# Four-block vision kernel: seven instead of six of sixteen scan states per tile have their input product on GpSimd, and the output evacuation moves behind the C copy of state 3

## The chip, the cores and the metric

The kernel runs on one core of a Trainium2 chip. The metric is the device time of one execution in microseconds (us), given as the median of several runs. Profiles come from one execution taken by the hardware profiler.

## What is computed

Four blocks follow each other on an image batch x of 4 x 32 x 32 x 32, each with a normalization in front and a residual sum behind: a deformable 3x3 convolution, a 7x7 neighbourhood attention, a three-direction selective scan (Mamba), and a convolution whose result is the sampling grid of a bilinear gather. The change touches only the third. Its core, cut from the reference:

```python
def mamba_dir(xz, conv_w, conv_b, x_proj_w, dt_w, dt_b, A_log, Dp):
    ...
    delta = softplus(einsum('dr,brl->bdl', dt_w, dt_raw) + dt_b)
    A = -exp(A_log)
    # for each of 16 states n, along the sequence l of 1024:
    #   h = h * exp(delta * A[n]) + (delta * u) * B[n];  y += h * C[n]
    y = selective_scan(x, delta, A, Bm, Cm) + Dp * x
    return y * silu(z)
```

## The kernel before, in words

Each engine has its own hand-written instruction stream, and the streams meet at counting semaphores; no scheduler reorders anything. The scan stage works through six tiles k = 0 to 5 (`DP`), three directions for each of two pairs of batch elements, in the order of `ORDER`. A tile is 128 rows by 1024 positions, and for each of its 16 states n (`NS`) the following happens:

- TensorE (`spread`, L880) replicates the rows B[n] and C[n] over the partitions with two 128x512 matmuls each. It does so for state n+4 before it sums state n (`AHEAD`, L939).
- ScalarE (loop at L1725) computes the decay exp(delta*A[n]) (L1729) and copies C out of PSUM banks 4 and 5 into a ring of four (L1742).
- VectorE multiplies du = delta*u with the B row in PSUM (`inject`, L1373, recorded at the helper's line L1061) and runs the recurrence as one scan instruction (`scan`, L1378, recorded at L1388).
- GpSimd (loop at L1877, all its multiplies recorded at L1789) multiplies the scan's result with C into a ring of four.
- TensorE (`collect`, L900) adds that product, transposed in eight matmuls, to the output y in banks 6 and 7.

States listed in `SHARED` (L63) go another way: their B row is replicated into the same banks 4 and 5 that the C rows use (`b_share`, L894, two states ahead), ScalarE copies it to SBUF (L1747), and GpSimd does the product with du, three states ahead (L1888). VectorE then has no `inject` for this state, only the scan. Banks 4 and 5 thus pass from TensorE to ScalarE once for each C row and once more for each shared B row, and each waits for the other at every passing. Two buffers hold shared products (`slot_free`, L78).

Extra work stands at fixed states. At state 8 ScalarE scales u by D (the "skip", L1752), which takes one more slot of the ring that the products go through. In tiles 0 to 2 GpSimd also computes du for a later tile behind state 7 (L1892). In tiles 1, 3 and 4 (`copy_y`, L1722) ScalarE evacuates the previous tile's output from banks 6 and 7 at state 3; in tiles 1 and 4 TensorE then transposes it back (`turn_back`, L924, matmuls at L929), ScalarE copies that in natural order at state 4 (L1738) and TensorE collects the copy (`collect_third`, L933).

Of the kernel before, what the change touches and what calls it, by code (L numbers as in the profile page):

```python
# [23 lines left out]
T = C * C  # L24
# [28 lines left out]
DI, NS, KC, RANK = 64, 16, 4, 2  # L53
DIRS, PAIRS = 3, 2
# [5 lines left out]
CGRP, CPER = 4, 8  # L60


SHARED = (3, 6, 8, 11, 13, 15)  # L63
NSH = len(SHARED)


ORDER = [PAIRS * dr + p for p in range(PAIRS) for dr in (2, 0, 1)]
# [5 lines left out]
def item(k, what):  # L73

    return ITEMS.index((k, what))


def slot_free(k, j):  # L78

    if j >= 2:  # L80
        return k * NS + SHARED[j - 2] + 1
    return (k - 1) * NS + SHARED[NSH - 1 - j] + 1


def injected(n):

    return sum(m not in SHARED for m in range(n + 1))

# [29 lines left out]
def above(n):  # L118
    return n + LEAD
# [17 lines left out]
def build(nc, d, out):  # L137
    with ExitStack() as ctx:
# [3 lines left out]
        def sem(name):  # L142
            return ctx.enter_context(nc.semaphore(name))
# [4 lines left out]
        def bank2(i):  # L148
            return ps[:, i:i + 2, :].rearrange("p a n -> p (a n)")
# [211 lines left out]
        def S(name):  # L361
            if name not in s:
                s[name] = sem(name)
            return s[name]
# [211 lines left out]
        def _(pe):  # L576
# [303 lines left out]
            def spread(k, n):  # L880

                t = ORDER[k]
                if n not in SHARED:
                    pe.wait_ge(S("scan"), above(k * NS + (n - 1)))
# [3 lines left out]
                pe.wait_ge(S("c_copied"), above(k * NS + n))  # L888
                if n + 1 in SHARED:
                    pe.wait_ge(S("b_copied"), above(k * NSH + SHARED.index(n + 1) + 1))  # L890
# [610 lines left out]
        def _(ac):  # L1501
# [40 lines left out]
            for k in range(TAPS):  # L1542
# [18 lines left out]
                if k in (2, 3):  # L1561

                    flat, n = off_px.rearrange("p c k n -> p (c k n)"), NBLK * NOFF // 3
# [158 lines left out]
            def copy_y(t, cols):  # L1722
                ac.activation(du[:, t, cols], bank2(6)[:, cols], ACT.Copy).then_inc(S("y_turned"), 1)

            for k in range(DP):  # L1725
                t = ORDER[k]
                for n in range(NS):
                    ac.wait_ge(S("scan"), above(k * NS + (n - 1)))
                    ac.activation(bank2(2 * (n % 2)) if n in SHARED else da[:, n % 2], delta[:, t], ACT.Exp,  # L1729
                                  scale=a_all[:, t * NS + n:t * NS + n + 1]).then_inc(S("da"), 1)  # L1730
                    if n == 3 and k in (1, DIRS, DIRS + 1):
                        ac.wait_ge(S("y_acc"), above(item(k - 1, NS - 1) + 1))
                        copy_y(0 if k == DIRS else ORDER[k - 1], slice(0, T))
                    if n == 4 and k % DIRS == 1:
                        q = item(k, "third")
                        ac.wait_ge(S("y_back"), 2 * (k // DIRS + 1))
                        ac.wait_ge(S("y_acc"), above(q - RING + 1))
                        ac.activation(hc_ring[q % RING].rearrange("p (s m) -> p s m", s=SLICES),  # L1738
                                      bank2(6).rearrange("p (m s) -> p s m", s=SLICES), ACT.Copy).then_inc(S("y_natural"), 1)
                    ac.wait_ge(S("c_rep"), above(k * NS + (n + 1)))  # L1740
                    ac.wait_ge(S("hc"), above(k * NS + (n - RING + 1)))
                    ac.activation(c_ring[n % RING], bank2(4), ACT.Copy).then_inc(S("c_copied"), 1)  # L1742
                    if n + 2 in SHARED:
                        j = SHARED.index(n + 2)
                        ac.wait_ge(S("b_share"), above(k * NSH + (j + 1)))
                        ac.wait_ge(S("scan"), above(slot_free(k, j)))
                        ac.activation(dbu_sh[j % 2], bank2(4), ACT.Copy).then_inc(S("b_copied"), 1)  # L1747
                    if n == SKIP_AT:
                        q = item(k, "skip")
                        ac.wait_ge(S("y_acc"), above(q - RING + 1))  # L1750
                        step = -1 if t // PAIRS == 1 else 1
                        ac.activation(hc_ring[q % RING], u[:, t // PAIRS, t % PAIRS, ::step], ACT.Copy,  # L1752
                                      scale=d_col[:, t // PAIRS, t % PAIRS:t % PAIRS + 1]).then_inc(S("skip"), 1)
# [271 lines left out]
```

## Time and profile before

| what | us |
|---|---|
| median of 3 runs (lowest, highest) | 751.73 (746.66, 754.73) |
| the profiled execution: its own time | 747.03 |
| the profiled execution: span from first to last instruction | 745.2 |
| busy over the span: VectorE, TensorE, ScalarE, GpSimd | 651.0, 605.2, 504.7, 418.9 |
| scan stage, 300.6 to 599.0: length | 298.4 |
| busy in it: VectorE, GpSimd, ScalarE, TensorE | 284.7, 262.3, 236.2, 209.8 |

In rows of the trace DVE is VectorE, ACT is ScalarE, POOL is GpSimd, PE is TensorE. A timeline row is: start in us from the span's start, length in us, engine, line, operation, output<-inputs, shape, count, and in brackets the idle time of the engine before it and what ended it. Instructions are pipelined, so the distance from one start to the next is often shorter than a length; the prediction goes by distances between starts. "PEclk" is the granted clock of TensorE as a share of 2.4 GHz.

### The profile page before, as it was taken

The numbers are of one execution on the slowest core, as the hardware profiler recorded it, in microseconds if no ns is written. First come the engines' busy times: TensorE is split into PE (matmuls) and PEld (weight loads), VectorE is DVE, ScalarE is ACT, GpSimd is POOL, SyncE is SP. The second block draws the span as 40 slices with busy tenths as digits, with TensorE's granted clock in tenths as the row PEclk, the third lists the DMA queues.
The fourth block names the chain that finished last, engine by engine and source line by source line (L and its number), as shares of the span: only waits on it lengthen the run. The fifth ranks groups of instructions, "written<-read, shape, count | busy, mean of one in ns | idle before, by whom it ended". The sixth has DMA issues, their size and how long they took to land.

```text
span 745.2 us, 11671 instructions
## 1 busy us (share of the span) xinstructions
PE 605.2 (81%) x3947; PEld 345.9 (46%) x3947; DVE 651.0 (87%) x900; ACT 504.7 (68%) x604; POOL 418.9 (56%) x288
## 2 busy tenths in 40 slices
PE   7899998999997971567676776777757789899997
PEld 5555545677774420245444454454434553333332
DVE  7899996879985979999999999999999874888876
ACT  2657531879984777688787787888877710577673
POOL 3788873000001067699899898798997920622321
PEclk9999999999999995599999898899997999899999
DMA  2004200341001032000000000000000013100000
GB/s 58 5 13 100 34 1 1 71 95 31 4 4 61 14 74 49 1 0 1 1 0 1 0 1 1 0 1 1 0 2 0 1 33 70 43 1 1 14 1 14
DMA packets 28853, 14.98 MB, mean 20 GB/s; under 512 B 23022, under 2 KB 24942, under 8 KB 28654
## 3 DMA queue, kind: packets, MB, share of 16 engines
q1 hardware_dynamic: 27582, 13.61, 8.3%
q10 hardware_dynamic: 1216, 0.66, 0.4%
q8 instruction: 32, 0.52, 0.3%
q14 instruction: 23, 0.19, 0.1%
HBM read 5.14 MB, written 0.78 MB: 8 GB/s over the span
## 4 chain that ended last, share of the span: by engine, by line
DVE 40%; PE 37%; ACT 10%; issue 9%; POOL 3%; DMA 0%; DVEq 0%; SPq 0%; ACTq 0%; POOLq 0%
PE ps L580 34%; DVE arena L1388 15%; DVE ps L1061 8%; DVE arena L1107 4%; DVE arena L1061 4%; ACT arena L1628 3%; ACT arena L1742 2%; DVE ps L1107 2%; PE ps L762 1%; DVE arena L1275 1%; POOL arena L1789 1%; DVE arena L1339 1%; ACT ps L1729 1%; PE ps L641 1%; ACT arena L1729 1%
## 5 line engine op out<-in xcount | busy, mean ns | idle before, releaser
L580 PE MATMUL ps<-arena 128*32 128x64 f32 (+5 forms) x2072 | 334.5, 350 | 111.1 <-ACT arena L1742 33.1
L580 PEld LDWEIGHTS ps<-arena 128*32 128x32 f32 (+4 forms) x2072 | 122.0, 123 | 242.4 <-issue 93.1
L1789 POOL TENSOR_TENSOR arena<-arena 128x1024 f32<-128x1024 f32 x87 | 173.8, 2012 | 32.3 <-DVE arena L1388 10.7
L1388 DVE TENSOR_TENSOR_SCAN arena<-arena,ps 128x1024 f32<-128x1024 f32 x60 | 137.2, 2286 | 8.2 <-DVE ps L1061 0.5
L1774 ACT ACTIVATE arena<-ps,nycol 128x1024 f32<-128x1024 f32 x64 | 71.1, 1113 | 55.3 <-PE ps L580 55.3
L1061 DVE TENSOR_TENSOR ps<-arena,ps 128x1024 f32<-128x1024 f32 x69 | 83.6, 1212 | 4.9 <-PE ps L580 3.9
L1388 DVE TENSOR_TENSOR_SCAN arena<-ps,arena 128x1024 f32<-128x1024 f32 x36 | 81.6, 2268 | 0.2
L1729 ACT ACTIVATE arena<-arena,a_col 128x1024 f32<-128x1024 f32 x60 | 68.6, 1144 | 10.9 <-DVE arena L1388 10.6
L1910 POOL TENSOR_TENSOR arena<-arena,bmask 128x128 f32<-128x128 f32 x64 | 30.7, 482 | 76.4 <-PE ps L580 65.3
L1061 DVE TENSOR_TENSOR arena<-ps,arena 128x512 f32<-128x512 f32 (+2 forms) x75 | 48.6, 654 | 23.5 <-PE ps L580 18.5
L1628 ACT ACTIVATE arena<-arena 128x256 f32<-128x256 f32 x128 | 59.0, 503 | 6.2 <-DVE arena L1275 4.7
L580 PE MATMUL ps<-ident,arena 128*128 128x128 f32 x416 | 58.8, 289 | 0.8 <-POOL arena L1789 0.8
L580 PEld LDWEIGHTS ps<-ident,arena 128*128 128x128 f32 x416 | 53.4, 151 | 11.8 <-issue 3.1
L1852 POOL MEMSET arena<- 128x6 f32 (+1 forms) x3 | 0.2, 101 | 101.0 <-DVE x2t L1302 101.0
L1747 ACT ACTIVATE arena<-ps 128x1024 f32<-128x1024 f32 x36 | 37.0, 1027 | 28.3 <-PE ps L580 28.3
L1742 ACT ACTIVATE arena<-ps 128x1024 f32<-128x1024 f32 x48 | 49.0, 1022 | 7.2 <-PE ps L580 7.1
L1275 DVE CUSTOM_DVE_ANT_0 arena<-ps,w_conv 128x256 f32<-128x256 f32 x124 | 50.9, 414 | 0.0
L1460 DVE TENSOR_SCALAR arena<-arena 128x1024 f32<-128x1024 f32 x64 | 46.9, 735 | 0.3 <-ACT arena L1774 0.3
L1729 ACT ACTIVATE ps<-arena,a_col 128x1024 f32<-128x1024 f32 x36 | 40.2, 1117 | 5.7 <-DVE arena L1388 5.7
L580 PE MATMUL ps<-arena,w_attn 96*128 96x512 bf16 (+1 forms) x132 | 42.5, 407 | 1.8 <-ACT arena L1774 0.9
L762 PE MATMUL ps<-ident,arena 128*128 128x128 f32 x256 | 38.4, 283 | 3.7 <-ACT arena L1628 2.3
L1107 DVE SCALAR_TENSOR_TENSOR arena<-ps,arena 128x1024 f32<-128x1024 f32 x32 | 37.0, 1217 | 3.1 <-ACT arena L1539 2.6
(208 smaller groups left out, 1016.4 us busy)
## 6 DMA issues: line engine op xcount, KB each, us to landing
arena<-arena SPq DMA_DIRECT2D x54, 64.0 KB
arena<-arena SPq DMA_DIRECT2D x12, 128.0 KB, 3.3
w_conv<-in_c_far SPq DMA_DIRECT2D x1, 1152.0 KB, 5.7
w_conv<-rpb_pad SPq DMA_DIRECT2D x36, 28.0 KB, 1.8
arena<-x SPq DMA_DIRECT2D x12, 64.0 KB, 2.0
arena<-x1t SPq DMA_DIRECT2D x12, 64.0 KB, 2.0
arena<-x3t SPq DMA_DIRECT2D x12, 64.0 KB, 2.0
arena<-arena SPq DMA_DIRECT2D x2, 288.8 KB, 3.7
```

Source lines behind the costliest of these rows:

```text
L580: return pe.matmul(o, l, r, start=start, stop=stop, **k)
L762: last = pe.transpose(ps[:, PT_BANKS[q % 2], side + P * c:side + P * c + P], pexp[:, (GROUP * g + e) % NRING, P * c:P * c + P], ident[:])
L1061: return ve.tensor_tensor(o, a, b, op)
L1107: return ve.scalar_tensor_tensor(out=square(o), in0=square(dx), scalar=0.0, in1=of, op0=sign, op1=ALU.mult)
L1275: ve.tensor_tensor_reduce(sc[:, n % NSB], ps[:, SC_BANKS[q % len(SC_BANKS)], SPAN * (e % 2):SPAN * (e % 2) + SPAN], bias(m, kind_of(i)), 1 ...
L1388: ve.tensor_tensor_scan(hs_ring[n % RING], decay, add, 0.0, ALU.mult, ALU.add).then_inc(S("scan"), 1)
L1460: ve.tensor_scalar(nhat[:, t % NU], ahat[:, t % NU], 1.0, 1.0, ALU.min, ALU.subtract).then_inc(S("nhat"), 1)
L1628: ac.activation(pexp[:, n % NRING], sc[:, n % NSB], ACT.Exp, bias=nmax[:, n % NSB:n % NSB + 1], scale=-1.0).then_inc(S("pexp"), 1)
L1729: ac.activation(bank2(2 * (n % 2)) if n in SHARED else da[:, n % 2], delta[:, t], ACT.Exp, scale=a_all[:, t * NS + n:t * NS + n + 1]).then ...
L1742: ac.activation(c_ring[n % RING], bank2(4), ACT.Copy).then_inc(S("c_copied"), 1)
L1774: ac.activation(ahat[:, t % NU].rearrange("p q n -> p (q n)"), bank2(2 * (t % 2)), ACT.Abs, bias=nycol[:, 0:1]).then_inc(S("abs"), 1)
L1789: return gp.tensor_tensor(o, a, b, ALU.mult)
```

## The change

`SHARED` gets seven states, every odd one from 3 on, instead of six, and in ScalarE's stream the evacuation of y (`copy_y`) at state 3 moves from ahead of the C copy to behind it.

```diff
-SHARED = (3, 6, 8, 11, 13, 15)
+SHARED = (3, 5, 7, 9, 11, 13, 15)
...
-                    if n == 3 and k in (1, DIRS, DIRS + 1):
-                        ac.wait_ge(S("y_acc"), above(item(k - 1, NS - 1) + 1))
-                        copy_y(0 if k == DIRS else ORDER[k - 1], slice(0, T))
...
                     ac.activation(c_ring[n % RING], bank2(4), ACT.Copy).then_inc(S("c_copied"), 1)
+                    if n == 3 and k in (1, DIRS, DIRS + 1):
+                        ac.wait_ge(S("y_acc"), above(item(k - 1, NS - 1) + 1))
+                        copy_y(0 if k == DIRS else ORDER[k - 1], slice(0, T))
```

ScalarE at states 3 to 5 of the fifth tile (k = 4), before: L1729 is a decay, L1723 the evacuation, L1742 a C copy, L1738 the copy in natural order, L1747 a copy of a shared B row.

```order
L1729 ACTIVATE ps<-arena,a_col 128x1024 [waits scan]
L1723 ACTIVATE arena<-ps 128x1024 [waits y_acc]
L1742 ACTIVATE x1t<-ps 128x1024 [waits hc,c_rep]
L1729 ACTIVATE arena<-arena,a_col 128x1024 [waits scan]
L1738 ACTIVATE arena<-ps 128x1024 [waits y_acc,y_back]
L1742 ACTIVATE arena<-ps 128x1024 [waits hc,c_rep]
L1747 ACTIVATE arena<-ps 128x1024 [waits scan,b_share]
```

The same place now (C copies are at L1739, the copy in natural order at L1735).

```order
L1729 ACTIVATE ps<-arena,a_col 128x1024 [waits scan]
L1739 ACTIVATE x1t<-ps 128x1024 [waits hc,c_rep]
L1723 ACTIVATE arena<-ps 128x1024 [waits y_acc]
L1747 ACTIVATE arena<-ps 128x1024 [waits scan,b_share]
L1729 ACTIVATE arena<-arena,a_col 128x1024 [waits scan]
L1735 ACTIVATE arena<-ps 128x1024 [waits y_acc,y_back]
L1739 ACTIVATE arena<-ps 128x1024 [waits hc,c_rep]
L1729 ACTIVATE ps<-arena,a_col 128x1024 [waits scan]
```

The evacuation stands behind the C copy of state 3, and the copy of a shared B row (that of state 5) now stands behind the evacuation; the one behind the C copy of state 4 (it was that of state 6) is gone.

TensorE at the start of the same tile, from the spread of state 3 to the spread of state 4, before: 128x512 pairs are replicated rows, 128x128 groups with "waits hc" a collect, those at L929 the turn-back.

```order
L580 MATMUL ps<-arena 128x512 [waits c_copied]
L580 MATMUL ps<-arena 128x512
L580 MATMUL ps<-ident,arena 128x128 [waits hc]
L580 MATMUL ps<-ident,arena 128x128 x7
L929 MATMUL ps<-ident,arena 128x128 [waits y_turned]
L929 MATMUL ps<-ident,arena 128x128 x7
L580 MATMUL ps<-arena 128x512 [waits scan]
```

The same place now.

```order
L580 MATMUL ps<-arena 128x512 [waits c_copied]
L580 MATMUL ps<-arena 128x512
L580 MATMUL ps<-arena 128x512 [waits c_copied]
L580 MATMUL ps<-arena 128x512
L580 MATMUL ps<-ident,arena 128x128 [waits hc]
L580 MATMUL ps<-ident,arena 128x128 x7
L929 MATMUL ps<-ident,arena 128x128 [waits y_turned]
L929 MATMUL ps<-ident,arena 128x128 x7
L580 MATMUL ps<-arena 128x512 [waits scan]
```

The shared B row of state 5 came in between the C row of state 3 and the collect of the previous tile's state 15, and it waits for the C copy of state 3, which the collect now waits for too.

GpSimd at states 0 to 5 of the second tile, before: rows that wait for "b_copied" are products of shared states, the others products with C.

```order
L1789 TENSOR_TENSOR x3t<-arena 128x1024 [waits c_copied,y_acc,scan,du_pool]
L1789 TENSOR_TENSOR arena<-arena 128x1024 [waits b_copied]
L1789 TENSOR_TENSOR xn<-arena 128x1024 [waits y_acc,c_copied,scan]
L1789 TENSOR_TENSOR arena<-arena,x 128x1024 [waits y_acc,c_copied,scan]
L1789 TENSOR_TENSOR arena<-arena,x1t 128x1024 [waits y_acc,c_copied,scan]
L1789 TENSOR_TENSOR arena<-arena 128x1024 [waits b_copied]
L1789 TENSOR_TENSOR x3t<-arena 128x1024 [waits y_acc,c_copied,scan]
```

The same place now.

```order
L1789 TENSOR_TENSOR x3t<-arena 128x1024 [waits c_copied,y_acc,scan,du_pool]
L1789 TENSOR_TENSOR arena<-arena 128x1024 [waits b_copied]
L1789 TENSOR_TENSOR xn<-arena 128x1024 [waits y_acc,c_copied,scan]
L1789 TENSOR_TENSOR arena<-arena,x 128x1024 [waits y_acc,c_copied,scan]
L1789 TENSOR_TENSOR arena<-arena 128x1024 [waits b_copied]
L1789 TENSOR_TENSOR arena<-arena,x1t 128x1024 [waits y_acc,c_copied,scan]
L1789 TENSOR_TENSOR x3t<-arena 128x1024 [waits y_acc,c_copied,scan]
L1789 TENSOR_TENSOR arena<-arena 128x1024 [waits b_copied]
```

From state 0 to state 12 a shared product now follows every second product with C.

## Rows read from the trace of the kernel before

**Rows 1.** Groups by line of VectorE, 299 to 600 us: busy, mean ns, idle before

```profile
L1061 DVE TENSOR_TENSOR ps<-arena,ps 128x1024 f32<-128x1024 f32 x60 | 72.6, 1210 | 4.3 <-PE ps L580 3.9
```

**Rows 2.** Timeline of VectorE: scan of state 0 of each tile, and last scan

```profile
300.58 2.29 DVE L1388 TENSOR_TENSOR_SCAN arena<-arena,ps 128x1024 f32<-128x1024 f32 x1
...
350.13 2.29 DVE L1388 TENSOR_TENSOR_SCAN arena<-arena,ps 128x1024 f32<-128x1024 f32 x1
...
399.71 2.29 DVE L1388 TENSOR_TENSOR_SCAN arena<-arena,ps 128x1024 f32<-128x1024 f32 x1
...
449.16 2.29 DVE L1388 TENSOR_TENSOR_SCAN arena<-arena,ps 128x1024 f32<-128x1024 f32 x1
...
499.23 2.29 DVE L1388 TENSOR_TENSOR_SCAN arena<-arena,ps 128x1024 f32<-128x1024 f32 x1
...
548.04 2.29 DVE L1388 TENSOR_TENSOR_SCAN arena<-arena,ps 128x1024 f32<-128x1024 f32 x1
...
596.65 2.28 DVE L1388 TENSOR_TENSOR_SCAN arena<-ps,arena 128x1024 f32<-128x1024 f32 x1
```

**Rows 3.** Timeline of VectorE: shared scan 11, product 12, shared scan 13, tile 0

```profile
335.17 2.26 DVE L1388 TENSOR_TENSOR_SCAN arena<-ps,arena 128x1024 f32<-128x1024 f32 x1
337.35 1.21 DVE L1061 TENSOR_TENSOR ps<-arena,ps 128x1024 f32<-128x1024 f32 x1
...
340.89 2.26 DVE L1388 TENSOR_TENSOR_SCAN arena<-ps,arena 128x1024 f32<-128x1024 f32 x1
```

**Rows 4.** Timeline of all engines: GpSimd's product for state 13 and its scan, tile 3

```profile
487.68 2.00 POOL L1789 TENSOR_TENSOR arena<-arena 128x1024 f32<-128x1024 f32 x1
...
489.64 2.00 POOL L1789 TENSOR_TENSOR arena<-arena,x1t 128x1024 f32<-128x1024 f32 x1
489.81 2.29 DVE L1388 TENSOR_TENSOR_SCAN arena<-ps,arena 128x1024 f32<-128x1024 f32 x1
```

**Rows 5.** Timeline, full clock: decay and C copy 6, shared B row, next rows

```profile
366.75 1.11 ACT L1729 ACTIVATE ps<-arena,a_col 128x1024 f32<-128x1024 f32 x1
...
367.78 1.01 ACT L1742 ACTIVATE x<-ps 128x1024 f32<-128x1024 f32 x1
...
368.86 0.60 PE L580 MATMUL ps<-arena 96*128 96x512 bf16 x2 [1.34 <-ACT x L1742]
...
369.50 1.03 ACT L1747 ACTIVATE arena<-ps 128x1024 f32<-128x1024 f32 x1 [0.70 <-PE ps L580]
...
370.17 1.09 PE L580 MATMUL ps<-arena 96*128 96x512 bf16 x4
```

**Rows 6.** Timeline, low clock: shared B row, next rows, product of state 10

```profile
377.46 0.76 PE L580 MATMUL ps<-arena 96*128 96x512 bf16 x2 [1.52 <-ACT arena L1742]
...
379.72 1.76 PE L580 MATMUL ps<-arena 96*128 96x512 bf16 x4
...
380.82 1.23 DVE L1061 TENSOR_TENSOR ps<-arena,ps 128x1024 f32<-128x1024 f32 x1 [0.25 <-PE ps L580]
```

**Rows 7.** Busy time by windows; behind POOL's come PEclk, DMA share, GB/s

```profile
377.80:381.20 3.40, 3.40 (x14) 2.33 (x13) 3.02 (x3) 2.06 (x2) 3.22 (x3) 0.50 0.00 0
```

**Rows 8.** Timeline of all engines, tile 4: decay 3, evacuation, turn-back, rows 4 and 5

```profile
505.16 1.11 ACT L1729 ACTIVATE ps<-arena,a_col 128x1024 f32<-128x1024 f32 x1
...
505.76 1.04 PE L580 MATMUL ps<-ident,arena 128*128 128x128 f32 x8
...
506.84 1.03 ACT L1723 ACTIVATE arena<-ps 128x1024 f32<-128x1024 f32 x1 [0.56 <-PE ps L580]
...
507.92 1.09 PE L929 MATMUL ps<-ident,arena 128*128 128x128 f32 x8 [1.12 <-ACT arena L1723]
...
508.85 1.03 PE L580 MATMUL ps<-arena 96*128 96x512 bf16 x4
...
513.88 1.03 PE L580 MATMUL ps<-arena 96*128 96x512 bf16 x4
...
514.52 1.23 DVE L1061 TENSOR_TENSOR ps<-arena,ps 128x1024 f32<-128x1024 f32 x1 [0.20 <-PE ps L580]
```

## The prediction

> **What bounds the kernel now.** I read the busy shares first, then the scan stage by engine, then single states. VectorE leads the busy shares, and the scan stage, where the change lies, keeps it busy almost throughout: the path runs there. In that stage its 60 input products cost 1.21 us each, and nearly all idle time ahead of them, 3.9 us, ended with a replicated row from TensorE [rows 1]. Next, the cadence of VectorE: from a shared scan to the next instruction 337.35 - 335.17 = 2.18 us, for a product with its scan 340.89 - 337.35 = 3.54 [rows 3]. A tile of ten unshared and six shared states needs 10 x 3.54 + 6 x 2.18 = 48.48. The first five tiles took 548.04 - 300.58 = 247.46, so they lost 247.46 - 5 x 48.48 = 5.06, about 1.0 each; I take the same for the sixth, 6.1 in all [rows 2].
>
> The other engines are close behind. GpSimd starts a multiply every 489.64 - 487.68 = 1.96 us, and VectorE's scan of a shared state follows 0.17 behind the end of its product (489.64 to 489.81): in the second half of this tile GpSimd, not VectorE, already came last [rows 4].
>
> **What the change takes away.** One product per tile leaves VectorE: 9 x 3.54 + 7 x 2.18 = 47.12, that is 1.36 per tile and 8.2 us over six tiles, if nothing else comes late. TensorE replicates as many rows as before. ScalarE gets one more B copy per tile and GpSimd one more multiply, both meant to lie beside VectorE's scans. Whether they do is the question.
>
> **What it adds on GpSimd.** In the alternation of shared and unshared states, VectorE needs 2.18 + 3.54 = 5.72 per pair, GpSimd 3 x 1.96 = 5.88. It starts a tile with some lead and loses 0.16 per pair. From the end of scan 2 to scan 11 VectorE needs four shared and four unshared states, 4 x 2.18 + 4 x 3.54 = 22.88. GpSimd has seven products with C (states 2 to 8) and four shared ones (5, 7, 9, 11): 11 x 1.96 plus two handovers of 0.17 is 21.9, in time. In tiles 0 to 2 the multiply for a later tile's du stands behind state 7: 23.9, so scan 11 comes 1.0 late, and the two pairs behind it lose 0.16 each. That makes 1.3 for a tile where nothing else is later: tile 2, and tile 0 (where I add 0.2 for its slow start). Tile 5 has no du multiply: 0.1.
>
> **What it adds between ScalarE and TensorE.** C rows and shared B rows pass through the same two banks in turn. At full clock, from a C copy's start to TensorE's next row 368.86 - 367.78 = 1.08, on to the B copy 0.64, and from the B row to the next state's B row, behind a collect, 370.17 - 368.86 = 1.31 [rows 5]; from that row to VectorE's product 514.52 - 513.88 = 0.64 [rows 8]. A pair costs ScalarE 1.72 from C copy to B copy and four more instructions of about 1.03 (decay 366.75 to 367.78 [rows 5]): 5.84, less some overlap of neighbours, about VectorE's 5.72. So lateness in this chain is not made up before state 14, whereas today the unshared pairs 4, 5 and 9, 10 give it room.
>
> **What it moves.** The evacuation has to stand behind the C copy of state 3 now: it waits for the collect of the previous tile's state 15, which TensorE issues behind the shared row of state 5, and that row waits for this C copy. In tile 4, counted from the scan of state 0 at 499.23 [rows 2]: decay 3 starts at 505.16, that is 5.93 [rows 8]; the C copy at 7.0; the B row of state 5 at 8.1 (+1.08); the collect 0.4 later, 8.5; the evacuation at 9.6 (505.76 to 506.84: 1.08); turn-back at 10.6 (506.84 to 507.92: 1.08); row of state 4 at 11.6 (0.93); its product at 12.2 (0.64). VectorE is ready for it after three unshared and one shared state less the first product, 499.23 + 11.47 = 510.70 by the cadence, so it waits 0.7. Queued behind the evacuation on ScalarE are the B copy of state 5, decay 4 and the copy in natural order; behind the turn-back on TensorE all later rows. The natural copy at 12.5 lets the third collect start at 13.5, the C row of state 5 at 15.3, its copy at 15.9, the B row of state 7 at 17.0, the row of state 6 at 18.3 and its product at 19.0, where VectorE would be at 17.9: another 1.0. Behind the skip at state 8 the same steps bring the row of state 10 about 0.8 late, decay 9 about 0.2, GpSimd's product for state 11 another 0.2, and the last two pairs 0.3. Together 3.2 for each of tiles 1 and 4 (in tile 1 the du multiply lies beside these waits). Tile 3 has the evacuation without the turn-back: the B copy of state 5 comes 1.8 late, and by the same steps VectorE loses 0.25 at state 6, 0.15 at decay 9, 0.8 at state 10, 0.2 at scan 11 and 0.3 in the last pairs, 1.7.
>
> **The clock.** At 377.80 to 381.20 the granted clock was 0.50, that is 1.2 GHz [rows 7]; just before, TensorE had waited 1.52 for a C copy [rows 6]. There, from the B row to the next row it took 379.72 - 377.46 = 2.26 instead of 1.31, and from there to the product 1.10 instead of 0.64 [rows 6]: 1.41 a round. Such stretches are part of the 1.0 lost per tile today; since nothing now catches up behind them, I add 2.0 for the stage, between 0 (the added B row at state 3 fills a pause of TensorE) and 8.5 (one more such round in every tile).
>
> **Sum.** Stalls after: 1.5 + 3.2 + 1.3 + 1.7 + 3.2 + 0.1 + 2.0 = 13.0, against 6.1 before: 6.9 given back out of 8.2, so -1.3. The profiled execution took 747.03, so 745.7. The median of the three runs is 4.7 above it, which I keep: 750.4. Everything outside the scan stage is unchanged.
>
> **Rivals.** Full gain: the chains run ahead as far as today, the stalls stay at 6.1 and the whole 8.2 is kept: 751.73 - 8.2 = 743.5. For it speaks that VectorE's only long waits are for TensorE's rows at unshared states, and state 5 has no such row any more; against it the cadence of GpSimd, above VectorE's in every pair. Chance 0.15.
>
> Slower: the clock falls twice in every tile. In the regular alternation TensorE stops before each shared B row until ScalarE has copied C, and these pauses recur in every pair; if TensorE falls to 1.2 GHz for two rounds per tile, that costs 12 x 1.41 = 16.9, 14.9 beyond my 2.0: 765.3. It decides from about six rounds beyond the allowance (6 x 1.41 = 8.5). For it speaks the low stretch of [rows 7], behind the skip's delay, a place that stays; against it that TensorE has as many rows to write in less time. The Trainium skill, "TensorE: Matmul & The Clock Gate", section "A second HAM failure mode: psum-queue depth-cycling", describes just this, short pauses between groups that cycle through PSUM banks making the clock swing; by that rule it would happen everywhere, while the row shows one stretch. Chance 0.14.
>
> GpSimd bound in all tiles: the ring of products holds its multiply of state 8 back in tiles 3 to 5 as the du multiply does in tiles 0 to 2. Then tiles 3 and 5 lose 1.3 more each, 753.0. For it speaks that scan 13 came behind GpSimd already in tile 3 [rows 4]; against it that the lead of 22.88 over 21.9 is there. Chance 0.13.
>
> **How the numbers follow.** The forecast has the remaining 0.58, with an own range of 746 to 755. A measurement of this kernel can tell about 1% from no change, that is below 744.2 or above 759.3. The full gain lies just below the first bound and counts about half, with a little from the forecast's edge: 0.10. The slower rival counts nearly whole, with a little of the forecast's upper edge: 0.15. The rest, 0.75, is within 1%. The range of 741 to 760 leaves out the larger part of the clock rival and a case where the old stalls go too.
>
> **What would show it.** In the changed profile: 54 input products instead of 60; tiles 1 and 4 longer than before, by about 48.81 to 49.58 before against 50.3, tiles 0, 2, 3 and 5 shorter by about a microsecond or more; a wait for TensorE ahead of the products of states 4 and 6 in tiles 1 and 4 and of state 10; scans 11, 13 and 15 behind GpSimd in tiles 0 and 2. I am wrong if tiles 1 and 4 get shorter, if all six lose or gain alike, or if low-clock stretches of TensorE spread over whole tiles.

## The result and the profile after

| what | us |
|---|---|
| before, median of 4 runs (lowest, highest) | 749.9 (746.66, 754.73) |
| after, median of 4 runs (lowest, highest) | 759.41 (756.78, 760.52) |
| after, the profiled execution: its own time, and its span | 760.52, 758.7 |

The ratio is 1.0136, with an interval from 1.0104 to 1.0167: the change makes the kernel slower by 1.4%. The profiled execution before took 747.03, so the two profiles are 13.5 apart. VectorE's tile starts, as in [rows 2], say where; the columns are start, length, engine and so on.

```profile
300.33 2.29 DVE L1388 TENSOR_TENSOR_SCAN arena<-arena,ps 128x1024 f32<-128x1024 f32 x1
...
351.65 2.29 DVE L1388 TENSOR_TENSOR_SCAN arena<-arena,ps 128x1024 f32<-128x1024 f32 x1
...
403.52 2.29 DVE L1388 TENSOR_TENSOR_SCAN arena<-arena,ps 128x1024 f32<-128x1024 f32 x1
...
452.25 2.29 DVE L1388 TENSOR_TENSOR_SCAN arena<-arena,ps 128x1024 f32<-128x1024 f32 x1
...
505.71 2.29 DVE L1388 TENSOR_TENSOR_SCAN arena<-arena,ps 128x1024 f32<-128x1024 f32 x1
...
557.98 2.29 DVE L1388 TENSOR_TENSOR_SCAN arena<-arena,ps 128x1024 f32<-128x1024 f32 x1
...
606.64 2.28 DVE L1388 TENSOR_TENSOR_SCAN arena<-ps,arena 128x1024 f32<-128x1024 f32 x1
```

| tile | 0 | 1 | 2 | 3 | 4 | 5, to its last scan | sum |
|---|---|---|---|---|---|---|---|
| before | 49.55 | 49.58 | 49.45 | 50.07 | 48.81 | 48.61 | 296.07 |
| predicted, the 2.0 for the clock left aside | 48.6 | 50.3 | 48.4 | 48.8 | 50.3 | | |
| after | 51.32 | 51.87 | 48.73 | 53.46 | 52.27 | 48.66 | 306.31 |

The scan stage is 10.2 longer, and the worst tile is 3. The other 3.5 or so lie behind it: from the last scan to the end it was 148.6 before and 152.1 after. They come up again at the end, where edits of the kernel before, with its six shared states, show a longer last stage too. Of the four tiles that the forecast had a microsecond or so shorter (0, 2, 3 and 5), only tile 2 is, by 0.7; tiles 0 and 3 got longer by 1.8 and 3.4.

The group of VectorE's input products, which answers to [rows 1], and its waits in the same stretch (waiting tensor and line, releaser, us in total, times, longest):

```profile
L1061 DVE TENSOR_TENSOR ps<-arena,ps 128x1024 f32<-128x1024 f32 x54 | 65.6, 1214 | 19.9 <-PE ps L580 19.7
```

```profile
DVE ps L1061 <- PE ps L580: 19.7, 14, 2.8
...
DVE arena L1388 <- ACT arena L1729: 0.9, 1, 0.9
```

Six products are gone, as meant. But the idle time ahead of those that are left, as far as it is put down to TensorE's rows, rose from 3.9 to 19.7, which is more than the 8.2 that the change takes away. GpSimd is not among the releasers.

The single waits, one instruction per row:

```profile
319.02 1.23 DVE L1061 TENSOR_TENSOR ps<-arena,ps 128x1024 f32<-128x1024 f32 x1 [1.41 <-PE ps L580]
...
332.84 1.23 DVE L1061 TENSOR_TENSOR ps<-arena,ps 128x1024 f32<-128x1024 f32 x1 [2.11 <-PE ps L580]
...
365.68 1.23 DVE L1061 TENSOR_TENSOR ps<-arena,ps 128x1024 f32<-128x1024 f32 x1 [2.47 <-PE ps L580]
...
473.29 1.23 DVE L1061 TENSOR_TENSOR ps<-arena,ps 128x1024 f32<-128x1024 f32 x1 [2.80 <-PE ps L580]
...
486.94 1.23 DVE L1061 TENSOR_TENSOR ps<-arena,ps 128x1024 f32<-128x1024 f32 x1 [2.09 <-PE ps L580]
...
517.91 1.23 DVE L1061 TENSOR_TENSOR ps<-arena,ps 128x1024 f32<-128x1024 f32 x1 [0.65 <-PE ps L580]
...
524.67 1.23 DVE L1061 TENSOR_TENSOR ps<-arena,ps 128x1024 f32<-128x1024 f32 x1 [0.93 <-PE ps L580]
...
538.64 1.23 DVE L1061 TENSOR_TENSOR ps<-arena,ps 128x1024 f32<-128x1024 f32 x1 [2.31 <-PE ps L580]
...
589.40 1.23 DVE L1061 TENSOR_TENSOR ps<-arena,ps 128x1024 f32<-128x1024 f32 x1 [2.13 <-PE ps L580]
```

By their distance from the tile starts there are two families: state 6 (or 4 and 6) in tiles 0, 1, 3 and 4, and state 10 in every tile: 2.11, 0.63, 0.99, 2.09, 2.31 and 2.13. Two short waits lie beside them, 0.31 at state 12 of tile 4 and 0.19 at state 6 of tile 5. Tile 5 shows the second family nearly alone, without evacuation and without a du multiply. Some rows of its timeline around the skip (L1752) of state 8, those of VectorE but one, GpSimd and the weight loads left out:

```profile
582.79 1.15 ACT L1752 ACTIVATE xn<-arena,d_col 128x1024 f32<-128x1024 f32 x1
...
583.83 1.12 ACT L1729 ACTIVATE ps<-arena,a_col 128x1024 f32<-128x1024 f32 x1
584.87 1.02 ACT L1739 ACTIVATE arena<-ps 128x1024 f32<-128x1024 f32 x1
...
585.95 1.03 PE L580 MATMUL ps<-arena 96*128 96x512 bf16 x2 [2.38 <-ACT arena L1739]
586.77 1.91 PE L580 MATMUL ps<-ident,arena 128*128 128x128 f32 x8
...
588.48 1.32 PE L580 MATMUL ps<-arena 96*128 96x512 bf16 x4
...
589.40 1.23 DVE L1061 TENSOR_TENSOR ps<-arena,ps 128x1024 f32<-128x1024 f32 x1 [2.13 <-PE ps L580]
```

The skip stands between two passings of banks 4 and 5. ScalarE copies C of state 9 at 584.87, and TensorE, which must put the B row of state 11 into the same banks, has nothing else ahead of that row in its stream: it waits 2.38. Then the row takes 1.03, the collect 1.91, and the row that VectorE wants comes 588.48 - 585.95 = 2.53 behind the B row, where it was 1.31 at full clock [rows 5]. The windows show the clock (columns: length, then busy time of PE, PEld, DVE, ACT and POOL, granted clock, DMA share, GB/s):

```profile
582.20:585.60 3.40, 0.97 (x6) 0.24 (x4) 3.27 (x3) 3.40 (x4) 2.94 (x2) 1.00 0.00 0
585.70:589.00 3.30, 3.06 (x12) 2.25 (x13) 1.57 (x1) 2.17 (x3) 0.14 (x1) 0.50 0.00 0
```

In the first window TensorE still has the full clock, with 0.97 of work in 3.40. In the next, where it has a backlog, it is at 0.50, that is 1.2 GHz. The same happens at the start of tile 3, this time ahead of the B row of state 5:

```profile
459.17 1.00 ACT L1739 ACTIVATE x1t<-ps 128x1024 f32<-128x1024 f32 x1
460.23 1.03 PE L580 MATMUL ps<-arena 96*128 96x512 bf16 x2 [2.75 <-ACT x1t L1739]
461.06 1.91 PE L580 MATMUL ps<-ident,xn 128*128 128x128 f32 x8
...
463.01 1.02 ACT L1723 ACTIVATE arena<-ps 128x1024 f32<-128x1024 f32 x1 [2.83 <-PE ps L580]
```

```profile
459.40:473.00 13.60, 10.39 (x36) 6.62 (x37) 10.12 (x5) 8.86 (x9) 10.15 (x6) 0.50 0.00 0
```

Here the low clock lasts for 13.6 us, and the moved evacuation (L1723) waits 2.83 for the slow collect, with the B copy queued behind it.

The pause alone does not bring the low clock about. TensorE waits 2.38 behind the skip in every one of the six tiles; in tile 1 the clock stayed at 1.00 behind it, and VectorE's product of state 10 waited 0.63:

```profile
382.48 0.61 PE L580 MATMUL ps<-arena 96*128 96x512 bf16 x2 [2.38 <-ACT arena L1739]
...
384.43 1.23 DVE L1061 TENSOR_TENSOR ps<-arena,ps 128x1024 f32<-128x1024 f32 x1 [0.63 <-PE ps L580]
```

```profile
380.80:384.20 3.40, 1.72 (x12) 1.22 (x12) 3.00 (x2) 2.70 (x4) 3.02 (x3) 1.00 0.00 0
```

Nor is a pause at the start of tile 3 new. In the kernel before, TensorE stood still there for 3.33, waiting for a scan, and the clock was low behind it too (459.7 to 466.5); but the collect of the previous tile's last state had run ahead of that pause:

```profile
454.22 1.04 PE L580 MATMUL ps<-ident,xn 128*128 128x128 f32 x8
...
458.59 1.04 PE L580 MATMUL ps<-arena 96*128 96x512 bf16 x4 [3.33 <-DVE arena L1388]
```

Apart from the stretch in which the scan stage begins, the granted clock stands at 0.50 in seven stretches of the stage before, 34 us together, and in ten of the change, 58 us together.

### The profile page after: what moved, and what is told of

It reads as the page before. It is cut to its first block, busy times and chain, and to the rows that moved or that the text cites. A ratio compares the mean times of both kernels' runs of the same rounds, so it can differ in the third digit from the quotient of the medians.

```text
span 758.7 us, 11689 instructions
## 1 busy us (share of the span) xinstructions
PE 618.2 (81%) x3947; PEld 353.6 (47%) x3947; DVE 646.5 (85%) x894; ACT 510.8 (67%) x610; POOL 430.7 (57%) x294
## 4 chain that ended last, share of the span: by engine, by line
PE 41%; DVE 30%; ACT 16%; issue 8%; POOL 3%; DMA 0%; DVEq 0%; SPq 0%; ACTq 0%; POOLq 0%
PE ps L580 38%; DVE arena L1388 9%; DVE ps L1061 5%; DVE arena L1107 4%; DVE arena L1061 4%; ACT arena L1628 3%; ACT arena L1739 3%; ACT ps L1729 2%; ACT x1t L1739 2%; DVE ps L1107 2%; ACT arena L1729 2%; POOL arena L1789 2%; PE ps L762 1%; DVE arena L1275 1%; ACT x L1739 1%
## 5 line engine op out<-in xcount | busy, mean ns | idle before, releaser
L580 PE MATMUL ps<-arena 128*32 128x64 f32 (+5 forms) x2072 | 341.4, 353 | 111.6 <-ACT arena L1739 37.6
L1789 POOL TENSOR_TENSOR arena<-arena 128x1024 f32<-128x1024 f32 x93 | 185.7, 2010 | 27.5 <-PE ps L580 8.8
L1388 DVE TENSOR_TENSOR_SCAN arena<-arena,ps 128x1024 f32<-128x1024 f32 x54 | 123.5, 2287 | 7.8 <-ACT arena L1729 0.9
L1774 ACT ACTIVATE arena<-ps,nycol 128x1024 f32<-128x1024 f32 x64 | 71.1, 1114 | 58.7 <-PE ps L580 58.5
L1388 DVE TENSOR_TENSOR_SCAN arena<-ps,arena 128x1024 f32<-128x1024 f32 x42 | 95.6, 2275 | 0.7
L1061 DVE TENSOR_TENSOR ps<-arena,ps 128x1024 f32<-128x1024 f32 x63 | 76.6, 1216 | 20.4 <-PE ps L580 19.7
L580 PE MATMUL ps<-ident,arena 128*128 128x128 f32 x416 | 64.4, 307 | 1.8 <-ACT arena L1735 0.9
L580 PEld LDWEIGHTS ps<-ident,arena 128*128 128x128 f32 x416 | 58.1, 162 | 14.4 <-issue 4.6
L1747 ACT ACTIVATE arena<-ps 128x1024 f32<-128x1024 f32 x42 | 43.1, 1026 | 31.5 <-PE ps L580 31.5
L1729 ACT ACTIVATE arena<-arena,a_col 128x1024 f32<-128x1024 f32 x54 | 61.7, 1143 | 3.5 <-DVE arena L1388 3.2
L1739 ACT ACTIVATE arena<-ps 128x1024 f32<-128x1024 f32 x48 | 49.0, 1020 | 4.9 <-PE ps L580 4.7
L1729 ACT ACTIVATE ps<-arena,a_col 128x1024 f32<-128x1024 f32 x42 | 46.9, 1117 | 4.5 <-DVE arena L1388 4.5
L762 PE MATMUL ps<-ident,arena 128*128 128x128 f32 x256 | 38.5, 283 | 3.7 <-ACT arena L1628 2.4
```

The lines of the kernel that those rows point to most:

```text
L580: return pe.matmul(o, l, r, start=start, stop=stop, **k)
L762: last = pe.transpose(ps[:, PT_BANKS[q % 2], side + P * c:side + P * c + P], pexp[:, (GROUP * g + e) % NRING, P * c:P * c + P], ident[:])
L1061: return ve.tensor_tensor(o, a, b, op)
L1388: ve.tensor_tensor_scan(hs_ring[n % RING], decay, add, 0.0, ALU.mult, ALU.add).then_inc(S("scan"), 1)
L1774: ac.activation(ahat[:, t % NU].rearrange("p q n -> p (q n)"), bank2(2 * (t % 2)), ACT.Abs, bias=nycol[:, 0:1]).then_inc(S("abs"), 1)
L1789: return gp.tensor_tensor(o, a, b, ALU.mult)
```

## The experiments

The theory is now: TensorE pauses at two places of a tile for a C copy of ScalarE (before the B row of state 5, and before that of state 11, behind the skip); the clock falls behind most of the longer pauses; the regular alternation leaves no place where the lateness is made up. The rivals: the moved evacuation costs the time by itself; GpSimd's du multiply and its short lead do; the skip's microsecond on ScalarE does, with the clock as a bystander. Where zero matmuls are added, they add zeros to y and change no output; in no run is work left out. The ratios are to the kernel before, each with its interval.

### The evacuation moved, six shared states

```diff
 SHARED = (3, 6, 8, 11, 13, 15)
...
-                    if n == 3 and k in (1, DIRS, DIRS + 1):
-                        ac.wait_ge(S("y_acc"), above(item(k - 1, NS - 1) + 1))
-                        copy_y(0 if k == DIRS else ORDER[k - 1], slice(0, T))
...
                     ac.activation(c_ring[n % RING], bank2(4), ACT.Copy).then_inc(S("c_copied"), 1)
+                    if n == 3 and k in (1, DIRS, DIRS + 1):
+                        ac.wait_ge(S("y_acc"), above(item(k - 1, NS - 1) + 1))
+                        copy_y(0 if k == DIRS else ORDER[k - 1], slice(0, T))
```

> The evacuation behind the C copy of state 3, with the six shared states of before. Pause theory (the loss is TensorE standing still before shared B rows at states 3 to 5 and behind the skip, and the 1.2 GHz that follows): no shared row waits behind the evacuation here, so the time stays within 3 us of the kernel before. Rival (the moved evacuation itself costs the time, because turn-back and the rows behind it come later): 5 to 10 us slower than before, with waits for TensorE at state 4 of tiles 1 and 4.

747.82, ratio 1.0013 (0.9984 to 1.0042). All tiles are within 0.1 of before (49.46, 49.58, 49.40, 50.06, 48.78, 48.63). The move alone costs nothing; it is the seventh state that does it, or both together.

### The change, with the skip at state 14

```diff
-SKIP_AT = NS // 2
+SKIP_AT = NS - 2
```

> The change, with the skip (ScalarE's scaling of u by D) behind state 14 instead of state 8, where no shared B row follows. Pause theory: the waits of 0.6 to 2.3 us before the product of state 10 (10.3 us over six tiles) nearly vanish, so 8 to 10 us less than the change: 749 to 752. GpSimd theory (GpSimd's 5.88 us per pair against 5.72 bounds the tiles): scans 11 and 13 come as late as now, at most 2 us less, 757 to 760.

752.73, ratio 1.0053 (1.0029 to 1.0077), 7 below the change. Tile 5 at state 9 now:

```profile
579.95 0.61 PE L580 MATMUL ps<-arena 96*128 96x512 bf16 x2 [1.34 <-ACT arena L1739]
...
581.27 1.09 PE L580 MATMUL ps<-arena 96*128 96x512 bf16 x4
...
582.28 1.21 DVE L1061 TENSOR_TENSOR ps<-arena,ps 128x1024 f32<-128x1024 f32 x1
```

The pause is 1.34 instead of 2.38, the row takes 0.61, the next comes 1.32 behind it, and VectorE waits for nothing. Over all tiles the waits at state 10 fell from 10.3 to 1.0, all of it in tile 1, but 2.1 came at state 12 of tiles 3, 4 and 5. The skip's place carries most of the state 10 family, but this run does not say whether by its own microsecond or by the clock.

### The change, with both pauses filled

```diff
                 last.then_inc(S("c_rep"), 1)
+                if k and n in (3, 9):
+                    for i in range(14):
+                        mm(ps[:, 6, 0:P], zeros[:], ident[:], start=False, stop=False, is_transpose=True, skip_group_check=True)
```

> The change, with 14 added 128x128 matmuls on TensorE (zeros added to y) before the shared B rows issued at states 3 and 9 of tiles 1 to 5, in the pauses. If the low clock behind the pauses is what costs: no low stretches at these two places, the product of state 10 waits 0.6 instead of 2.1, and tiles 1, 3 and 4 lose less at states 4 to 6: 6 to 10 us less than the change, 749 to 754. If the pauses alone cost and the clock only follows them: no gain, 758 to 762.

753.16, ratio 1.0066 (1.0049 to 1.0083), 6 below the change; the stage is 297.09, 9.2 shorter. The skip stands where the change has it:

```profile
576.51 1.69 PE L581 MATMUL ps<-ident,zeros 128*128 128x128 f32 x14
...
579.06 0.60 PE L581 MATMUL ps<-arena 96*128 96x512 bf16 x2 [0.85 <-ACT arena L1743]
...
580.37 1.09 PE L581 MATMUL ps<-arena 96*128 96x512 bf16 x4
...
581.01 1.23 DVE L1065 TENSOR_TENSOR ps<-arena,ps 128x1024 f32<-128x1024 f32 x1 [0.31 <-PE ps L581]
```

The row of state 11 still waits for the same copy, but the clock has stayed up (row 0.60, distance 1.31), and VectorE's wait is 0.31 instead of 2.13. So in tile 5 the skip's microsecond is worth 0.31 and the clock 1.8, of which 1.50 is the way from the B row to the product (581.01 - 579.06 = 1.95 against 589.40 - 585.95 = 3.45). Other waits did not all go: at state 10 there stayed 0.62, 0.23, 0.62 and 0.63 in tiles 1 to 4, and 1.37 in tile 0, which has no zeros; at state 12 of tiles 1, 3 and 4 there are 0.97, 1.04 and 1.06, each at a granted clock of 0.50. In all, eight low stretches are left besides the first, 27 us together instead of 58.

Not all of the 9.2 is due to the zeros. Tile 0 is 2.3 shorter (49.04) without any: there the low clock in which the stage begins ended at 314.0 instead of 319.4, and state 6 did not wait. The other 6.9 lie in tiles 1 to 5.

### The change, with the du multiply at state 14

```diff
-                    if n == 7 and k < DIRS:
+                    if n == 14 and k < DIRS:
```

> The change, with GpSimd's du multiplies of tiles 0 to 2 behind state 14 instead of state 7. GpSimd theory: scan 11 of these tiles comes 1.0 us earlier and the next two pairs 0.3, 3 to 4 us less than the change: 756. Pause theory: the product of state 10 waits for TensorE in these tiles anyway, so less than 1 us: 759.

760.11, ratio 1.015 (1.0106 to 1.0193): no gain. GpSimd's du multiply falls as a cause of this loss. The profile shows something else: at state 10, tile 1 now waits 2.31 instead of 0.63, and tile 5, whose instructions the edit leaves as they were, 0.99 instead of 2.13. Which tile the low clock hits differs between the two profiles, so a single tile's loss is not to be read too closely.

### Skip at 14, and the pause at state 3 filled

```diff
-SKIP_AT = NS // 2
+SKIP_AT = NS - 2
...
+                if k and n in (3,):
+                    for i in range(14):
...
```

> The change with both: the skip behind state 14, and 14 added matmuls of zeros before the shared B row issued at state 3 of tiles 1 to 5. If the pauses at the two places and the low clock behind them account for the whole loss, what is left is the change's gain less the evacuation's delay: 744 to 749, no slower than the kernel before. If a third thing (GpSimd's cadence) holds the tiles: 751 or more.

749.41, ratio 1.0 (0.9974 to 1.0026); the stage takes 295.6. With both places mended the loss is gone, but 8.2 are not won:

```profile
DVE ps L1065 <- PE ps L581: 8.8, 12, 1.4
...
DVE arena L1392 <- POOL arena L1793: 1.6, 3, 0.5
```

Now GpSimd does come last, 0.5 for each of three tiles.

### Controls: the same two edits on the kernel before

```diff
 SHARED = (3, 6, 8, 11, 13, 15)
...
-SKIP_AT = NS // 2
+SKIP_AT = NS - 2
```

> The kernel before, with the skip behind state 14 instead of state 8. Tells whether the skip's place costs anything without the change. If ScalarE's chain through banks 4 and 5 has slack at states 9 and 10 there (two unshared states): at most the 1.9 us of waits before the product of state 10 goes, 745 to 748. If moving the skip is worth the 7 us that it was worth behind the change: 741.

750.4, ratio 1.0004 (0.9978 to 1.0031): the waits of state 10 (0.25, 0.81 and 0.83) go, and those at state 5, which were 0.94, 0.83 and 0.20 in tiles 0, 2 and 4, are 1.03, 0.97 and 2.04, with 0.58 more in tile 5.

```diff
 SHARED = (3, 6, 8, 11, 13, 15)
...
+                if k and n in {9: 14}:
+                    for i in range({9: 14}[n]):
...
```

> The kernel before with 14 matmuls of zeros before the shared B row issued at state 9 of tiles 1 to 5, a control for the added matmuls. The waits of 0.8 us before the product of state 10 (tiles 3 and 5) came with a low clock: if the clock is their cause they go, 746 to 748; if not, no difference or slower, 749 to 752. In no case the 6 us that the matmuls were worth behind the change.

750.01, ratio 1.0023 (1.0002 to 1.0045): again no gain. The profiled execution, at 754.95 the longest of the ten, has waits at state 5 of up to 2.7. So what these edits give the changed kernel is no gift that any kernel would take. It fits that before, the two unshared pairs caught the lateness, but that is not shown.

### Seven shared states in another order

```diff
-SHARED = (3, 6, 8, 11, 13, 15)
+SHARED = (3, 6, 8, 10, 12, 14, 15)
```

> Seven shared states as in the change, but at 3, 6, 8, 10, 12, 14 and 15, with the evacuation where the kernel before has it: no shared row is issued at state 3, and at state 8 the copy of the shared row stands ahead of the skip. Pause theory: the waits at states 4 and 6 of tiles 1, 3 and 4 are gone (about 9 us less than the change), those at state 10 stay or move to state 11 and 12: 746 to 753. If seven shared states cost the time wherever they stand: 757 to 762.

767.8, ratio 1.0244 (1.0192 to 1.0296), far from the 746 to 753 that the expectation gave. States 4 and 5 are unshared here, so no shared row is issued at state 3, but the skip stands inside the alternation as in the change, and VectorE waits behind it at states 9, 11 and 13. That is not all: 7.3 of the 22.9 are at state 5, ahead of the skip, where the expectation had none.

```profile
L1061 DVE TENSOR_TENSOR ps<-arena,ps 128x1024 f32<-128x1024 f32 x54 | 65.7, 1217 | 22.9 <-PE ps L580 22.9
```

The same order of states with the skip at state 15:

```diff
-SKIP_AT = NS // 2
+SKIP_AT = NS - 1
```

> The same seven states (3, 6, 8, 10, 12, 14, 15) with the skip behind state 15. Pause theory: both pauses gone, most of the 8.2 us of VectorE's work is kept: 741 to 746, faster than the kernel before. If GpSimd's cadence holds the tiles: 748 or more.

755.86, ratio 1.0084 (1.0057 to 1.0112): 12 less, which is the skip's place again, but not the 741 to 746 expected. Of the waits for TensorE 4.7 are at state 5 again. The waits now come from three engines:

```profile
DVE ps L1061 <- PE ps L580: 7.0, 8, 1.9
...
DVE arena L1388 <- POOL arena L1789: 3.8, 6, 1.3
DVE arena L1388 <- ACT ps L1729: 3.2, 5, 0.8
```

The waits for GpSimd and ScalarE lie for 6.2 of their 7.0 at states 14 and 15, two shared states in a row. That these two cost what the order saves in the middle is read from the profile and was not tried apart.

### Towards a version that beats both

First the evacuation's chain, on the kernel with skip 14 and state 3 filled: the evacuation goes behind the B copy of state 5, the turn-back behind the spread of state 4, the natural copy behind the C copy of state 4.

```diff
                         ac.activation(dbu_sh[j % 2], bank2(4), ACT.Copy).then_inc(S("b_copied"), 1)
+                    if n == 3 and k in (1, DIRS, DIRS + 1):
+                        ac.wait_ge(S("y_acc"), above(item(k - 1, NS - 1) + 1))
+                        copy_y(0 if k == DIRS else ORDER[k - 1], slice(0, T))
...
+                    if k * NS + n + AHEAD < DP * NS:
+                        spread(*divmod(k * NS + n + AHEAD, NS))
                     if k % DIRS == 1 and n == 0:
```

> As the version with the skip behind state 14 and matmuls of zeros at state 3, and the evacuation's chain made shorter: ScalarE evacuates behind the copy of state 5's shared row, TensorE turns back behind the rows of state 4, and the copy in natural order stands behind the C copy of state 4. If the waits of 0.6 and 0.9 us before the products of states 4 and 6 in tiles 1 and 4, and that at state 8 of tile 3, come from the evacuation: 2 to 4 us less than that version, 744 to 747. If other waits take their place: 748 to 751.

748.32, ratio 0.9995 (0.998 to 1.0011), the expectation's second branch, in which other waits take the place of those mended. Tile 3 falls from 49.49 to 47.26, close to the floor of the cadence (47.12); but tiles 1 and 4 take 51.59, with waits of up to 3.3 at state 6. Then six zero matmuls ahead of each later shared row:

```diff
-                if k and n in {3: 14}:
+                if k and n in {3: 14, 5: 6, 7: 6, 9: 6, 11: 6, 13: 6}:
```

> The same, with six matmuls of zeros more in each of the short pauses before the shared rows issued at states 5, 7, 9, 11 and 13. If low-clock stretches still cost (waits at states 8, 12 and 14): none left in tiles 1 to 5, 2 to 4 us less than without, 741 to 745. If the added matmuls delay the rows themselves: more time than without them.

746.17, ratio 0.9965 (0.9945 to 0.9986), a microsecond above the 741 to 745 expected. The waits for TensorE shrink to four, and GpSimd comes last in four tiles, three of which have a du multiply:

```profile
DVE ps L1065 <- PE ps L581: 7.7, 4, 3.3
...
DVE arena L1392 <- POOL arena L1793: 1.9, 4, 0.6
```

Last, that multiply behind state 15:

```diff
-                    if n == 7 and k < DIRS:
+                    if n == 15 and k < DIRS:
```

> The same, with GpSimd's du multiplies behind state 15 instead of 7. If scan 11 of tiles 0 to 2 now waits for GpSimd (0.5 us each): 1 to 2 us less than without, 740 to 744. If GpSimd had slack: no difference.

743.45, ratio 0.9928 (0.9898 to 0.9959), which beats both kernels, the one before by 0.7%. No wait for GpSimd is left, and tiles 2 and 3 are at the floor, 47.15 each:

```profile
401.12 2.29 DVE L1392 TENSOR_TENSOR_SCAN arena<-arena,ps 128x1024 f32<-128x1024 f32 x1
...
448.27 2.29 DVE L1392 TENSOR_TENSOR_SCAN arena<-arena,ps 128x1024 f32<-128x1024 f32 x1
...
495.42 2.29 DVE L1392 TENSOR_TENSOR_SCAN arena<-arena,ps 128x1024 f32<-128x1024 f32 x1
```

What is left are four waits for TensorE: two of 1.42 and 1.01 in tile 0, which has no zeros, and two behind the third collect in tiles 1 and 4. In tile 4, at a granted clock of 1.00, the wait is 1.68; in tile 1, where that collect ran at 0.50 (364.0 to 367.4), it is the longest:

```profile
371.14 1.23 DVE L1065 TENSOR_TENSOR ps<-arena,ps 128x1024 f32<-128x1024 f32 x1 [3.32 <-PE ps L581]
```

## Why the prediction was wrong

The forecast was 750.4, "within 1%"; the kernel takes 759.41 and is slower. What came is nearest to the rival "the clock falls twice in every tile", with 765.3 somewhat too dear and with its place partly wrong. The start of the sum was off as well: it took 751.73, the median of three runs, and later rounds of the same kernel had medians of 748.1 to 748.8 from 25 or 26 runs; from there the forecast would have been about 747, and the miss larger.

- **What the change takes away** was right: 54 products instead of 60, and a floor of 47.12 per tile. No tile of the change reaches it, but tiles 2 and 3 of the last experiment do, with 47.15.
- **The clock is the step that failed.** I allowed 2.0 for the stage, between 0 and 8.5, and held against the rival that TensorE has as many rows to write in less time and that the row shows one stretch. [rows 7] is one of seven in the stage before; the change has ten, and 58 us of low clock instead of 34. By tile, the first five of the change lose 22.05 against the floor (257.65 - 5 x 47.12), and my terms for them without the allowance are 10.9: the miss is 11.15, of which 2.70 lie in tile 0, 1.55 in tile 1, 0.31 in tile 2, 4.64 in tile 3 and 1.95 in tile 4. With the two pauses filled they lose 15.0 (250.61 - 235.6), 7.0 less. Of these, 2.3 are tile 0's, which has no zeros; 4.8 lie in tiles 1 to 4, and tile 5 gives back 2.2 besides. So TensorE having work in its pauses, and the clock that stays up with it, is worth 6.9 in the five tiles that have the zeros, where I had 2.0 for all six.
- **My chain had the queue, but not its clock.** In tile 4 the collect behind the added B row starts 8.48 behind the tile's first scan (514.19 - 505.71), where I had 8.5. In tile 3 it is 8.81 (461.06 - 452.25), against 5.06 before (454.22 - 449.16). What the chain lacked is that in tile 3 this collect and the rows behind it run at 0.50, 1.91 instead of 1.04; and the added row does not fill the pause, of which 2.75 are left. Tile 1 against tile 4 shows the same: the wait at state 4, for which I gave 0.7, is 2.47 where the clock was low (360.4 to 367.2) and 0.65 where it was not. The Trainium skill, "TensorE: Matmul & The Clock Gate", section "A second HAM failure mode: psum-queue depth-cycling", warns of short pauses between groups that cycle through PSUM banks. That agrees with the 2.38 and 2.75 in front of low stretches here, but the length of a pause does not tell: the 2.38 of tile 1 kept the full clock; the regular pauses of 1.34 kept it in tile 5 with the skip at 14, while with the pauses filled one of 1.34 in tile 4 stands in front of a stretch at 0.50 (535.8 to 539.2).
- **The rest of the miss**, 4.1, is what the first five tiles lose beyond my terms even with the pauses filled. Of it 2.3 lie in tile 3, which I put at 1.7 beyond the floor: it still loses 4.00, with waits at states 8, 10 and 12 (1.21, 0.62, 1.04), nearly as much as tiles 1 and 4 with the turn-back (4.17 and 4.10). The first and the last of these waits come in stretches at 0.50 (471.0 to 474.4 and 484.6 to 488.0), so the clock has a part in them too. The experiment that moved the evacuation behind the B copy brought tile 3 from 49.49 to 47.26, which shows that its place matters; that tile then had one low stretch instead of two, and the two shares were not told apart.
- **The evacuation's chain** in tiles 1 and 4 was right in place and size where the clock was up: I gave 0.7 at state 4 and 1.0 at state 6, tile 4 had 0.65 and 0.93, and tile 1 with the pauses filled 0.66 and 0.94. At state 10 I gave 0.8; with the pause filled it was 0.62 and 0.63, in tile 4 of the change 2.31, the clock on top. For the last two pairs I gave 0.3; with the pauses filled, state 12 alone waited 0.97 and 1.06, at low clock.
- **GpSimd's 1.3** in tiles 0 and 2 did not show: VectorE waits for TensorE before it comes to scan 11, and that gives GpSimd time. Its multiply moved away from the change brings nothing; it shows as 0.5 a tile only when the other waits are mended. My bound was a real limit, but the sum counted it beside waits that hid it. The row from which I took GpSimd to come last before, the scan at 489.81 in [rows 4], began 2.27 behind the scan before it, where VectorE's own cadence is 2.2: at most 0.1 was GpSimd's.
- **Full gain** would have needed the chains to run ahead as far as before. They do not. That the two unshared pairs 4, 5 and 9, 10 were what caught lateness is argued, not shown: in the two controls a mended wait at state 10 brought nothing and the waits at state 5 grew, which fits, but the order that kept 4 and 5 unshared waited 7.3 at state 5 as well.

What stays open is what sets the clock: why it stayed up behind the pause of 2.38 in tile 1, and why it stays low for 13.6 us in tile 3. That tile 2 loses only 1.6 in the change goes with a shorter pause at state 3, 1.34 instead of the 2.75 of tiles 1, 3 and 5: its low stretch came sooner (404.7 to 408.2). Why it came there is open too.

## What to carry to other kernels

An order of work that is perfectly regular is also one with no slack: before making an alternation tighter, look for the extra instructions that stand inside it (here one scale, one evacuation, one du multiply) and move them to a stretch that has room. Where an engine hands two PSUM banks back and forth with TensorE, a row moved earlier in TensorE's queue can hold back ready work instead of filling a pause; ask which copy it waits for and what is queued behind. And price a pause of TensorE not by its length but by what the queue behind it costs at half clock, if a low stretch already stands behind such a pause in the trace of before; count these stretches over the whole stage, one row does not tell how many there are.

## What the runs showed that was not expected

Filling a pause with work that computes nothing made the kernel faster: 14 transposes of zeros at two places in five of the six tiles took 6 off the change, although they stand ahead of a row on which VectorE waits.

The length of the sampling stage, which no edit touches, differs between profiles. From the last scan to the end the kernel before took 148.6 and the moved evacuation 148.5; the other twelve profiles, the change and two edits of the kernel before with six states among them, took 150.4 to 152.1. Where the time goes is ScalarE's copies at L1774, which waited 55.3 for TensorE in the profile before and 58.5 now:

```profile
L1774 ACT ACTIVATE arena<-ps,nycol 128x1024 f32<-128x1024 f32 x64 | 71.1, 1114 | 58.7 <-PE ps L580 58.5 <-DVE arena L1460 0.2
```

In the change the low clock lies over the stage's first matmuls, and in the kernel before it came sooner, 37 instead of 44 behind the last scan, beside GpSimd's work on the coordinates; that it cost less there is read from these rows. First the window of the change, then that of the kernel before:

```profile
650.60:657.30 6.70, 5.66 (x9) 2.45 (x10) 2.94 (x5) 1.17 (x2) 2.35 (x5) 0.50 0.16 43
```

```profile
633.80:640.60 6.80, 5.56 (x9) 1.64 (x8) 6.03 (x6) 2.81 (x4) 6.57 (x5) 0.50 0.28 75
```

So a difference of 3.5 between two profiles of this kernel can come from there, whatever was edited. The runs without a profile divide as well: of the 26 of the kernel before in the last round, the 13 with a mean granted clock of 0.943 or 0.944 took 746.7 to 748.0, and the 13 with 0.932 to 0.939 took 748.8 to 751.7. That this is the same stage is not shown.
